# Four gated decoder layers on one core: first routing placed inside its mixture, statistics taken early and the residual joined within the last block attention

## The reference

```python
x = x + tanh(g_xattn[0]) * L0_xattn(layernorm(x), ctx, ctx)
x = x + tanh(g_ffn[0])   * L0_ffn(layernorm(x))
...
x = x + tanh(g_xattn[3]) * L3_xattn(layernorm(x), ctx, ctx)
x = x + tanh(g_ffn[3])   * L3_ffn(layernorm(x))
```

```python
scores = softmax(xt @ gate_w.T); weights, idx = top_k(scores, 2)
xs = xt[:, None, :] * weights[:, :, None]
for e in range(8):
    h  = silu(xs @ w1[e].T + b1[e])
    x2 = h @ w2[e].T + b2[e]
    x3 = xs @ w3[e].T + b3[e]
    y += sum(x2 * x3 * (idx == e))
return y + silu(xt @ sw1.T) * (xt @ sw2.T) @ sw3.T
```

```python
ln1 = layer_norm(hidden, ln1_weight, ln1_bias)
qkv = ln1 @ qkv_weight.T
ao  = causal_attention(qkv)            # 16 heads over 4 groups
h1  = hidden + ao @ proj_weight.T
ln2 = layer_norm(h1, ln2_weight, ln2_bias)
return h1 + experts(ln2, top_2(softmax(ln2 @ router_weight)))
```

## Time and profile before

| | us |
|---|---|
| median of three executions | 3067.46 (3067.04 to 3073.78) |
| the profiled execution, its own time | 3074.13 |
| span of its trace | 3072.3 |
| TensorE busy (PE) | 2775.6, 90% of the span |
| VectorE busy (DVE) | 2027.8, 66% |
| ScalarE busy (ACT) | 1842.9, 60% |
| GpSimd busy (POOL) | 1431.1, 47% |

### The profile page before, as it was taken

The page is one execution under the profiler, slowest core; times in us unless marked ns, Lnnn a source line. Parts: engine busy times, 40 slices in busy tenths (PEclk is TensorE's granted clock), DMA queues, the critical chain, the costliest instruction groups (busy, mean ns, idle before and its releaser), DMA issues. The chain is left out here.

```text
span 3072.3 us, 70587 instructions
## 1 busy us (share of the span) xinstructions
PE 2775.6 (90%) x21912; PEld 2135.0 (69%) x21912; DVE 2027.8 (66%) x7991; ACT 1842.9 (60%) x5350; POOL 1431.1 (47%) x1748
## 2 busy tenths in 40 slices
PE   7999979986999989999999999988899884597999
PEld 5888854433767668888888877666667662486776
DVE  5445536664653456666666559999999999686433
ACT  5777734443545256666666468888888874453333
POOL 2221217772542434444444248787878786452000
PEclk9999979997999999999999899999999995697999
DMA  3000014423755311111111000000000000001000
GB/s 115 6 5 6 5 43 96 82 50 118 261 215 179 96 49 55 55 55 55 54 53 54 19 10 14 14 14 14 14 14 14 14 14 33 3 18 36 8 10 10
DMA packets 99582, 152.03 MB, mean 49 GB/s; under 512 B 11360, under 2 KB 39536, under 8 KB 98864
## 3 DMA queue, kind: packets, MB, share of 16 engines
q1 hardware_dynamic: 99392, 149.96, 16.5%
HBM read 103.33 MB, written 46.47 MB: 49 GB/s over the span
## 5 line engine op out<-in xcount | busy, mean ns | idle before, releaser
L1896 POOL TENSOR_TENSOR l2a_probs<-l2a_probs,l2a_inv 128x1024 f32<-128x1024 f32 x128 | 242.5, 1895 | 370.6 <-DVE l2a_inv L2062 370.4
L2007 ACT ACTIVATE l2a_probs<-l2a_s_ps,l2a_nm 128x256 f32<-128x256 f32 x512 | 236.6, 473 | 200.5 <-DVE l2a_nm L2038 200.5
L2844 DVE MAX8 l3a_top<-l3a_work 128x8 f32<-128x128 f32 x1536 | 316.9, 291 | 0.0
L2421 POOL TENSOR_SCALAR l3a_above<-l3a_score,l3a_top 128x128 f32<-128x128 f32 x504 | 295.4, 603 | 16.7 <-DVE l3a_top L2844 7.3
L2562 PE MATMUL l3a_l2o_ps<-net_arena 128*128 128x128 f32 x1952 | 250.4, 291 | 35.9 <-ACT net_l1f_gate L2678 35.3
L2562 PEld LDWEIGHTS l3a_l2o_ps<-net_arena 128*128 128x128 f32 x1952 | 243.0, 206 | 48.6 <-ACT net_l1f_gate L2678 38.7
L2846 DVE MATCH_REPLACE8 l3a_work<-l3a_top,l3a_work 128x128 f32<-128x128 f32 x1024 | 270.7, 290 | 0.0
L2549 PE MATMUL l3a_l2h_ps<-net_cols,net_arena 128*128 (+1 forms) x1024 | 253.9, 390 | 15.5 <-ACT net_arena L2713 13.7
L2549 PEld LDWEIGHTS l3a_l2h_ps<-net_cols,net_arena 128*128 128x128 f32 x1024 | 185.5, 192 | 69.5 <-ACT net_arena L2713 27.3
L721 ACT ACTIVATE l0a_probs<-l0a_score_ps,l0a_nm 128x128 f32<-128x128 f32 x512 | 180.1, 382 | 74.7 <-DVE l0a_nm L770 74.7
L2713 ACT ACTIVATE net_arena<-l3a_l2h_ps,net_l2f_b 128x256 f32<-128x256 f32 x496 | 203.8, 494 | 12.5 <-PE l3a_l2h_ps L2549 11.2
(11 more groups left out here) (531 smaller groups left out, 7184.3 us busy)
## 6 DMA issues: line engine op xcount, KB each, us to landing
kv_ahead<-l1a_kept SPq DMA_DIRECT2D x128, 256.0 KB, 2.6
l0f_code<-code_rows SPq DMA_DIRECT2D x32, 512.0 KB, 10.9
l2a_kT<-kv_ahead SPq DMA_DIRECT2D x64, 256.0 KB, 2.6
l2a_v<-kv_ahead SPq DMA_DIRECT2D x64, 256.0 KB, 2.6
l1a_shift<-neg_top SPq DMA_DIRECT2D x16, 512.0 KB, 4.9
keys_ahead<-l1f_keys_kept SPq DMA_DIRECT2D x32, 256.0 KB, 2.2
l1f_chosen<-mask_code SPq DMA_DIRECT2D x64, 128.0 KB, 3.2
l3a_kT<-keys_ahead SPq DMA_DIRECT2D x32, 256.0 KB, 2.7
```

Of the source, the lines that this page charges most:

```text
L1896: pool.tensor_tensor(p[:, :, :], p[:, :, :], per_row(inv[c % 2][a][:, :, :].rearrange("p i o -> p (i o)"), KV), ALU.mult).then_inc(scaled, 1)
L2007: act.activation(probs[c % 2][a][:, 2 * i + odd, :], s_ps[a][odd][:, i * KV:(i + 1) * KV], ACT.Exp, bias=nm[c % 2][a][:, i, odd:odd + 1], ...
L2421: ins = pool.tensor_scalar(above[:, i, :], score[c % 4][:, h, :], top[c % 2][:, ROUNDS - 1, h, 7:8], None, ALU.is_ge)
L2844: ins = dve.max(t[:, step // 2, h, :], src)
```

## The change

Four things are altered.

- **Routing of layer 0** is no longer a stage. Its DVE operations, ScalarE's exponential and TensorE's transposes of the code stand at the head of the programs in `l0_mixture`. The shared expert of the first AHEAD = 4 groups is done there too, before any expert: TensorE's 24 products with the code's transposes between them (the code takes `y_ps`), both evacuations on ScalarE, the product of the two on POOL (`shared_ahead`), the sum's evacuation on ScalarE (`sum_ahead`). The code is stored by group, 8 DMAs; the loads of group 0 wait for the first of them only. Groups 4 to 7 run as before.
- **Statistics before block attention.** In the drain of l3a, DVE takes the statistics of tiles 0 to 11 and then 12 to 30 (`measure_rows`), and the moments of half 0; POOL makes the powers of half 0. `normalise_twice` replaces `normalise` for n3f: one statistic, moments and powers of half 1, staging, and kept rows, of which ScalarE does four groups (five before). The kept rows are also written to `residual_rows` in DRAM.
- **Block attention** loads the residual by position (4 DMAs of 512 KB, each into 32 partitions), POOL adds it to a step's rows (`join`, lag 3, ahead of `shift`), DVE takes their statistics into six more columns (`measure`, lag 3, ahead of `divide`). Rows of 134 numbers (536 bytes) are stored with lag 3, from four buffers. 28 steps (112 positions) and step 28 (4 positions) are taken back after its store; the last three steps go from SBUF straight into `attended`, four DMAs each.
- **n3m** is `normalise_measured` on `attended` with the statistics that came with it; it has 24 warming transposes and powers in four parts of eight tiles. The gated addition to `net_x` is now one DVE operation a group in `last_mixture` (`join`).

```diff
 def l0_mixture(nc, k):
+    AHEAD = 4
...
+                keep(0)
                 for g in range(NG):
                     i = g % 2
+                    if g == 1:
+                        for later in range(1, NG):
+                            keep(later)
+                        for later in range(1, NG):
+                            sp.wait_ge(code_kept[later], 16)
+                    if g == 0:
+                        sp.wait_ge(code_kept[0], 16)
...
+                def shared_ahead(g, c):
+                    n = g * SH + c
+                    pool.wait_ge(silu_done, n + 1)
+                    pool.wait_ge(x3_kept, n + 1)
+                    if g >= 2:
+                        pool.wait_ge(x2_mm, g - 1)
+                    pool.tensor_tensor(s_hidden[g % 2][:, c, :], x3[c][:, :], s_gate[g % 2][:, c, :], ALU.mult
+                                       ).then_inc(ahead_ready, 1)
...
+                for n in range(AHEAD * SH):
+                    first(n)
+                    if n == 4:
+                        turn_code(0)
+                    if n % SH == 0 and n:
+                        second(n - 1)
+                        if n == 4:
+                            turn_code(1)
+                        if n == 6:
+                            for g in (2, 3, 4):
+                                turn_code(g)
+                for g in (5, 6, 7):
+                    turn_code(g)
+                second(AHEAD * SH - 1)
...
 def l3_attention(nc, k):
+                def measure_rows(q, c):
+                    early = 12
+                    tiles = range(early, NB - 1) if c == NB - 1 else range(early)
+                    for t in tiles:
+                        dve.wait_ge(x_done, t + 1)
+                        dve.bn_stats(k.stats[:, t, :], k.x[:, t, :]).then_inc(k.late.measured, 1)
+                        if t == NB // 2 - 1:
+                            dve.wait_ge(k.late.measured, NB // 2)
+                            row_moments(dve, link, k, slice(0, NB // 2))
...
+def normalise_twice(nc, k, name, gains, gain, shift):
...
+                for g in range(NG):
+                    tiles = slice(g * G4, (g + 1) * G4)
+                    if g < kept_by_act:
+                        sp.wait_ge(kept_act, G4 * (g + 1))
+                    else:
+                        sp.wait_ge(kept_dve, G4 * (g - kept_by_act + 1))
+                    sp.dma_start(k.residual_rows[tiles].rearrange("b p d -> p b d"), k.rows[:, tiles, :]
+                                 ).then_inc(k.residual_out, 16)
...
+                link(dve.bn_stats(k.stats[:, NB - 1, :], k.x[:, NB - 1, :]))
+                row_moments(dve, link, k, halves[1])
+                make_shift(0)
...
 def l3_block_attention(nc, k):
+    RW, TAIL = D + 6, 3
-        y = [s.sb(f"y{i}", [P, D]) for i in two]
+        y = [s.sb(f"y{i}", [P, RW]) for i in range(4)]
+        residual = s.sb("residual", [P, P // PJ, D])
...
+                sp.wait_ge(k.residual_out, 16 * NG)
+                for j in range(PJ):
+                    sp.dma_start(residual[S * j:S * j + S, :, :],
+                                 k.residual_rows[:, :, :].rearrange("s (c j) d -> s j c d", j=PJ)[:, j, :, :]
+                                 ).then_inc(residual_in, 16)
...
+                    if isinstance(q, int) and q * BODY + c >= NN - TAIL:
+                        for j in range(PJ):
+                            at = first_position(q, c) + j
+                            sp.dma_start(k.attended[at:at + 1, :, :], y[c % 4][S * j:S * j + S, :]
+                                         ).then_inc(att_in, 16)
+                        return
...
                 def take_most():
-                    stored(NN - BODY)
+                    stored(NN - TAIL)
                     take_back(0, NN - BODY)
-                schedule(sp, [(store, 2)], take_most)
-                stored(NN)
-                take_back(NN - BODY, NN)
-                sp.wait_ge(att_in, 32)
+                    take_back(NN - BODY, NN - TAIL)
+                schedule(sp, [(store, 3)], take_most)
+                sp.wait_ge(att_in, 32 + 16 * PJ * TAIL)
...
-                schedule(pool, [(gather, -2), (shift, 0)])
+
+                def join(q, c):
+                    if isinstance(q, int) and q * BODY + c == 0:
+                        pool.wait_ge(residual_in, 16 * PJ)
+                    wait(pool, y_ready, q, 1, c + 1)
+                    rows = residual[:, ds(q * BODY + c, 1), :].rearrange("p o d -> p (o d)")
+                    pool.tensor_tensor(y[c % 4][:, 0:D], y[c % 4][:, 0:D], rows, ALU.add).then_inc(y_joined, 1)
+                schedule(pool, [(gather, -2), (join, 3), (shift, 0)])
...
-                schedule(dve, [(soften, 0), (take_k, -1), (take_v, -1), (divide, 1)])
+
+                def measure(q, c):
+                    wait(dve, y_joined, q, 1, c + 1)
+                    dve.bn_stats(y[c % 4][:, D:RW], y[c % 4][:, 0:D]).then_inc(y_measured, 1)
+                schedule(dve, [(soften, 0), (take_k, -1), (take_v, -1), (measure, 3), (divide, 1)])
...
 def last_mixture(nc, k, name, ...):
+                def join(g):
+                    tiles = ds(g * G4, G4)
+                    dve.scalar_tensor_tensor(out=k.x[:, tiles, :], in0=k.attended[:, tiles, 0:D], scalar=gate,
+                                             in1=k.x[:, tiles, :], op0=ALU.mult, op1=ALU.add).then_inc(joined, 1)
```

More of the change, by code:

```diff
@@ L231, in place_weights, with row_moments @@
     f.rows = f.add(part(0, NB, D), d["ctx"].rearrange("b p d -> p b d"))
+def row_moments(dve, link, k, some):
+    late = k.late
+    dif, mean, var, veps, veps2 = (t[:, some] for t in (late.dif, late.mean, late.var, late.veps, late.veps2))
+    even_mean, even_m2, odd_mean, odd_m2 = (k.stats[:, some, i] for i in (1, 2, 4, 5))
+    link(dve.tensor_tensor(dif, even_mean, odd_mean, ALU.subtract))
+    link(dve.tensor_tensor(var, even_m2, odd_m2, ALU.add))
+    link(dve.tensor_tensor(mean, even_mean, odd_mean, ALU.add))
+    link(dve.scalar_tensor_tensor(out=dif, in0=dif, scalar=0.25, in1=dif, op0=ALU.mult, op1=ALU.mult))
+    link(dve.tensor_scalar(mean, mean, 0.5, None, ALU.mult))
+    link(dve.scalar_tensor_tensor(out=var, in0=var, scalar=1.0 / D, in1=dif, op0=ALU.mult, op1=ALU.add))
+    dve.tensor_scalar(veps2, var, 1.0 + LN_EPS, LN_EPS * LN_EPS, ALU.mult, ALU.add).then_inc(late.veps_ready, 1)
+    dve.tensor_scalar(veps, var, LN_EPS, None, ALU.add).then_inc(late.veps_ready, 1)
@@ L534, in _ @@
             def _(act):
-                if gain is not None:
+                if gains is not None:
                     gains.wait(act)
@@ L894, in l0_mixture @@
         code = [s.sb(f"code{i}", [P, E, BANK]) for i in two]
[L895 to L896 removed]
+        xsT, hidden, x3, z = ([s.sb(f"{n}{i}", [P, BANK]) for i in two] for n in ("xsT", "hidden", "x3", "z"))
+        acc = [s.sb(f"acc{i}", [P, BANK]) for i in range(AHEAD)]
+        s_gate, s_hidden = ([s.sb(f"{n}{i}", [P, SH, BANK]) for i in two] for n in ("s_gate", "s_hidden"))
+        code_turned = code[1][0:E, :, :]
         h_ps, x3_ps, x2_ps, y_ps = ([s.ps(f"{n}{i}", [P, BANK]) for i in two] for n in ("h", "x3", "x2", "y"))
@@ L2099, in last_mixture @@
             "stored"))
+        joined = s.sem("joined")
         with nc.Block() as block:
@@ L2926, in l3_block_attention @@
         att_in = s.sem("att_in")
-        y_stored = [s.sem(f"y_stored{i}") for i in two]
+        y_stored = [s.sem(f"y_stored{i}") for i in range(4)]
+        residual_in, y_joined, y_measured = (s.sem(n) for n in ("residual_in", "y_joined", "y_measured"))
         (filled, made, staged, k_mm, v_mm, q_ready, k_ready, v_ready, s_mm, s_out, maxed, shifted, exped,
@@ L3184, in program @@
         k.measured = s.sem("measured")
+        k.late = Shared()
+        k.late.dif, k.late.mean, k.late.var, k.late.veps, k.late.veps2, k.late.rstd, k.late.rstd2 = (
+            s.sb(f"late_{n}", [P, NB]) for n in ("dif", "mean", "var", "veps", "veps2", "rstd", "rstd2"))
+        k.late.measured, k.late.veps_ready, k.late.rstd_ready = (
+            s.sem(f"late_{n}") for n in ("measured", "veps_ready", "rstd_ready"))
         k.x_in = [s.sem(f"x_in{i}") for i in range(4)]
```

333 lines of the change are left out of this document (226 added, 107 removed).

## The result

The changed kernel took 3031.79 us (median of four executions, 3022.21 to 3032.19), the kernel before 3068.05 (3067.04 to 3073.78): by the medians 36 us less, where 22 were forecast, and 5 us below the range's lower end of 3037. The ratio is given as 0.9867, with a 95% interval of 0.9854 to 0.988. Two more sets of executions of the same code on other occasions gave 0.9892 (0.9865 to 0.992) and 0.9892 (0.9863 to 0.9921); all thirteen executions lie between 3022 and 3043 us, with a median of 3032.3. The profiled execution took 3032.19 us, its span is 3030.4 us.

What follows compares the result with a forecast made beforehand. TensorE was taken as nearly always at work (104.3 of 106.2 us in block attention), except in serial heads and a tail. Savings of 4.0, 7.5, -0.5, 1.0 and 10.0 make 22.0 us: 3067.46 to 3045.5 us, range 3037 to 3056.

Steps and rivals of the forecast that it cites:

- Rivals 1 to 4: A giving nothing back (0.15), 536-byte rows slow (0.08), DVE bounding the step (0.08), residual late (0.05 half rate, 0.03 quarter).
- A: Layer 0's routing inside the mixture, shared expert of four groups ahead: 4.0 us saved, ends -4 and 10.
- B: Statistics and powers taken before block attention, in n3f: 7.5 us saved, ends 6 and 8.5.
- D: Normalisation n3m before the last mixture, additions and statistics gone: 10.0 us saved, ends 9 and 11.
- the tail: Rows' way back after block attention, next stage at 2802.5 against 2803.7: 1.0 us saved, ends 3 and -4.
- the same helper in layer 0, 25.4 us: Whole length of layer 0's normalisation, set against n3m's 35.5 us to get the 10.0 us saving.
- Rival 5: Layer 0's mixture gains more, POOL at 2.75 us: 3039 us in all, chance 0.03.
- C: Additions and statistics inside block attention's 32 steps, PE staying the bound: -0.5 us, ends 0 and -5.
- rivals 2 and 4: In block attention: 536-byte rows slow, 3050.5 (0.08); residual loads late, 3054.8 at half rate (0.05), 3080 at a quarter (0.03).
- + 1: After block attention: 1 us for the take-back's last four positions and 12 small DMAs, in 2790 + 11.5 + 1.

Runs made afterwards that it cites:

- warm0: The changed kernel with no warming transposes in n3m in place of 24; 3044.29 us, n3m 25.3 us.
- tail0_warm40: The changed kernel with 40 warming transposes in n0f and n2f, and block attention's last four steps through DRAM as in the kernel before; 3028.5 us.
- warm40: The changed kernel with 40 in place of 24 warming transposes in n0f and n2f; 3026.78 us, and 3027.82 in a second copy.

## Why the prediction was wrong, point by point

Rivals 1 to 4 did not come, and the savings of A, B and D came by the ways described. But D had a second cause that I had left out, the clock, A was sized at less than half, the tail had the wrong sign, and the range had no width for the clock of stages that do not change. Only D lies outside its ends in the first trace; A is close to its upper end of 10.

- **D, 10.0, measured 17.4 in the first trace (20.7 us left, so 14.8, in the second; 11.7 to 17.5 over all traces).** The step that failed is "the same helper in layer 0, 25.4 us": it took n0f's length as its work. It was that of an execution in which the clock fell early. The windows table shows the half clock in its own column; I used it for layer 0's head and not for the row that I took as a price. At half clock the forecast comes within 0.2 us (warm0), in part by luck, as n0f's 25.4 us held 5.4 us at full clock and warm0's n3m none. What the runs show in place of the 10.0 is some 10 us of work and 1.5 to 7 of clock. The end of 11 was 6.4 us too low.
- **A, 4.0, measured 9.5 at group 4, 9.2 to 12.7 for the stage.** I had worked out 4.8 and entered 4.0; of the other 4.7 us, the head took 1.3 less than I had; the weighings came at 2.86 and not 2.95 (31 times, 2.8 us); and I counted the first of them from the start of the first expert's product, though it lies 2.0 us ahead of it (450.86 against 452.84), as the two buffers of `xsT` allow. The last step was 1.4 longer. DVE and POOL did meet in the head, but it was DVE that waited: the routing step that takes 0.42 us in the kernel before took 1.37 (at 428.31, where POOL's product takes 1.39), and the mask was 2.3 us later. Rival 5 (6.5 us better than the forecast, chance 0.03) came nearer by its sum, though not by its rate of 2.75.
- **B, 7.5, measured 8.1.** All steps came within 1 us: staging after 1.86 us (forecast 2.04), and an idle of 0.96 us left on POOL (0.5).
- **C, -0.5, measured about -0.1 in the loop, -0.5 with the head.** The residual was in time and the rows of 536 bytes cost nothing, so that rivals 2 and 4 fall, the latter also at half rate: the four loads of 512 KB landed in a median of 8.0 us each from their issue, all by 2648.72, 12.7 us after the first issue (forecast 12.6), and POOL's first use is at 2654.63. The Trainium skill's rule on rows off a 256-byte boundary (DMA: Bandwidth & Descriptors, "How a descriptor splits into AXI transactions") does not show in the time of this transfer. I had made a factor of 1.5 of it, though the Trainium skill's example there, 25 beats against 18, makes 1.39 by the same estimate.
- **Tail, +1.0, measured -2.7.** That the take-back must await step 28 came true: it left 2.3 us before the last row was taken out, and 4.6 before it in the kernel before. The sum in the text was 1.2 and not 1.0. The failing term is "+ 1" for the second part and the twelve: from the first take-back's issue to the next stage are 16.4 us, of which it lands in some 11 (11.1 in tail0_warm40), so 5 in place of 1. SP's second issue alone held SP for 5.1 us, and the twelve followed at 0.67 each. Whether it is this issuing or the moving that costs the 5 us stays open.
- **Missing: the clock of unchanged stages.** The median before, 3067.46, was 6.7 us under the profiled execution, and a difference such as n0f's (8.2 us) could explain that distance; only one execution of the kernel before in that set has a trace, so it is not shown. I carried the saving over to the median, which was right, but gave the range no width for the clock. Thirteen executions of the changed kernel spread over 20 us here.

By stages, over all traces, A 9.2 to 12.7, B 7.5 to 8.1, C and tail -1.9 to -3.1 and D 11.7 to 17.5 make 25 to 36 us; the medians moved by 33 to 36. More than that the spread of the executions does not let one tell apart.

## To carry to other kernels

A stage's length in one trace is not its work: read the granted clock in the row before it is used as a price, and give two numbers where the clock decides. Let warming work reach up to the first real tile: here a pause of 1.8 us behind it went with 6 us more in n2f, one of 6.45 us with 7 more in n3m. When work is pulled ahead of a loop, ask which engine then sets the loop's pace without it (here POOL, by its busy time); doing half of it ahead was worth as much here.

## What the runs showed of the hardware that I had not expected

- Some 120 instructions of TensorE in n0f, the same in both kernels, take 17.3 to 25.5 us, by where the clock falls among them; before it fell in the changed kernel's n0f, TensorE had been busy 12.86 of 14.80 us.
- Useless transposes shorten a kernel: 64 more in n3m of the kernel before, 7.1 us less of that stage; 16 more in n0f and in n2f of the kernel before, 8 us less by the medians (3059.87 against 3067.82; 1 to 10 by the interval).
- 384 rows of 536 bytes from SBUF to SBUF, behind a large transfer, were through sooner as twelve transfers of 32 rows than as three of 128 (14.1 and 16.4 us from the last row to the next stage, one trace with the three). With the three, the DMA engines were busy 0.28 of the time over 7 us of it.
- TensorE's clock falls with TensorE at work: in warm40's n0f it was busy 10.34 of the 10.60 us before the fall.
